# A fused attention and expert layer on one core: the shared MLP of two batches of eight moved behind the experts

## The chip, the cores and the metric

One core of a Trainium2 chip runs the whole program in one launch. The time is device microseconds (us). PE is the matmul engine, ACT (ScalarE), DVE (VectorE) and POOL (GpSimd) are the three others that compute, and SP only issues DMAs. Each engine takes its instructions in the written order, so one that waits holds up all behind it.

## The reference, cut to what matters

Eight batches of 1024 rows with 256 numbers pass through an attention layer and then this (T = 8192 rows, 16 experts, C = 1024 rows for each):

```python
    scores = jax.nn.softmax(flat_x @ gate_w.T, axis=-1).T
    topk_weight, topk_idx = jax.lax.top_k(scores, C)
    xg = flat_x[topk_idx]
    h = gelu(einsum('ecd,eid->eci', xg, Wg)) * einsum('ecd,eid->eci', xg, Wu)      # I = 1024
    eo = einsum('eci,edi->ecd', h, Wd) * topk_weight[..., None]
    flat_out = zeros_like(flat_x).at[topk_idx.reshape(-1)].add(eo.reshape(-1, d))
    shared = gelu(flat_x @ Sg.T) * (flat_x @ Su.T) @ Sd.T                          # IS = 512
    x = x + _layernorm(out + shared)
```

## The kernel before, in words

Four stages follow each other, each a block of its own with a barrier at its end: attention, the shared MLP, the experts and the output. `mlp` (line 1038) is written for both MLPs.

The shared MLP works in halves of 512 rows, 16 of them. A half has four up steps (`step`, one for 128 of the 512 hidden columns): PE makes 12 matmuls for G and U (each product in three, high and low parts of both operands), ACT takes the gelu of G, DVE multiplies it with U out of PSUM (line 1322), ACT rounds the product to its high part (1257) and DVE subtracts for the low part (1308, `part_lo`). Then `down` multiplies with Sd in four tiles of 128 rows, psD has two buffers, and ACT takes each tile out (1288). SP stores it to ACC in DRAM. The order on all engines is: steps 0 and 1, and then for each half its steps 2 and 3, steps 0 and 1 of the next half, and `down` of this one. Steps are numbered through, 64 in all.

Beside it `TopK` (line 679) finds the 1024 rows of each expert. It has a table for each engine that says after which step a piece runs. 30 bits of the threshold are found one after another: DVE counts (788), PE sums over partitions (793), DVE updates (798, 800). A count stands after each step from 3, so four in a half. At step 34 come the masks (865), then ranks (934), slots (940 to 946) and digits (951, 953) in steps 36 to 41, and from step 42 the lists: for each of eight chunks DVE writes lo1 twice (975), hi1 twice (965) and val (988, 989), POOL writes the other half of val (776), and PE multiplies them (1004). POOL then writes the lists to DRAM and reads them back as indices.

The experts stage has 16 experts with two halves each of eight up steps and a `down` of eight matmul groups per tile. POOL gathers rows by index, and adds the result to ACC with an indirect DMA for each tile (1443). SP loads the weights.

The output stage (`output`, line 1459) takes pairs of batches. SP loads F from ACC (1490). DVE takes statistics of 16 tiles (1525), aggregates them (1528) and computes scale and shift in a chain of 12 instructions on 16 numbers per partition (63 to 75, `layernorm_scale`). ACT normalises (1556), POOL adds the residual X1 in halves of 128x1024 (1569), and SP stores. The last batch is normalised and added on DVE (1543, 1546).

## Time and profile before

| what | value |
|---|---|
| time, three runs | 2233.16, 2235.63 (median), 2236.29 us |
| profiled execution, first to last instruction | 2228.4 us |
| PE busy | 2048.3 us (92%) |
| DVE, ACT, POOL busy | 1227.1, 994.6, 448.8 us |
| PE's matmuls of the shared MLP | first 688.4, last 1021.1 us |
| PE's matmuls of the experts | first 1037.8, last 2147.4 us |
| output stage | to 2228.4 us |

The profiled execution's own time outside the trace isn't given; its span stands 7.2 us under the median of the runs. Matmuls are pipelined and their listed durations overlap, so the pace of PE is read from the distance of starts. A row of a timeline with "x16" is 16 instructions merged, with the time from the first start to the last end.

### The profile page before, as it was taken

The numbers are of one execution on the slowest core, as the hardware profiler recorded it, in microseconds if no ns is written. First come the engines' busy times: TensorE is split into PE (matmuls) and PEld (weight loads), VectorE is DVE, ScalarE is ACT, GpSimd is POOL, SyncE is SP. The second block draws the span as 40 slices with busy tenths as digits, with TensorE's granted clock in tenths as the row PEclk, the third lists the DMA queues.
The fourth block names the chain that finished last, engine by engine and source line by source line (L and its number), as shares of the span: only waits on it lengthen the run. The fifth ranks groups of instructions, "written<-read, shape, count | busy, mean of one in ns | idle before, by whom it ended". The sixth has DMA issues, their size and how long they took to land. (4 is left out here: it accounts for less than half of the span.)

```text
span 2228.4 us, 34450 instructions
## 1 busy us (share of the span) xinstructions
PE 2048.3 (92%) x12462; PEld 1800.2 (81%) x12464; DVE 1227.1 (55%) x2535; ACT 994.6 (45%) x1854; POOL 448.8 (20%) x391
## 2 busy tenths in 40 slices
PE   7999999999967999886999999999999999999950
PEld 6888888888855888775888888888888888888840
DVE  5586667567564776993453443534435344353438
ACT  4464565566433434223443443434434344344415
POOL 0000000000001000233123232232322323223115
PEclk9999999999988999998999999999999999999985
DMA  2011011010013111103233333333333333333247
GB/s 107 1 39 59 39 77 58 39 56 39 40 77 124 58 56 57 38 29 137 72 75 76 88 75 76 86 62 89 75 75 85 63 87 75 76 85 63 69 113 282
DMA packets 53987, 165.74 MB, mean 74 GB/s; under 512 B 6657, under 2 KB 23233, under 8 KB 46689
## 3 DMA queue, kind: packets, MB, share of 16 engines
q1 hardware_dynamic: 29104, 129.13, 15.7%
q0 software_dynamic: 24752, 34.75, 9.7%
q8 instruction: 97, 1.59, 0.3%
q14 instruction: 34, 0.27, 0.0%
HBM read 104.55 MB, written 59.31 MB: 74 GB/s over the span
## 5 line engine op out<-in xcount | busy, mean ns | idle before, releaser
L1322 DVE TENSOR_TENSOR ex_HF<-ex_psU,ex_GL 128x512 f32<-128x512 f32 x256 | 177.1, 692 | 619.1 <-ACT ex_GL L1263 619.1
L1443 POOL DMA_INDIRECT ACC<-ex_OUT,ex_GI x128 | 200.2, 1564 | 710.0 <-ACT ex_OUT L1288 682.0
L1263 ACT ACTIVATE ex_GL<-ex_psG 128x512 f32<-128x512 f32 x256 | 153.4, 599 | 358.7 <-PE ex_psU L56 358.7
L54 PE MATMUL ex_psD<-ex_wd_hi,ex_H_hi 128*128 128x256 f32 x1024 | 289.8, 283 | 0.2 <-DVE ex_H_lo L1308 0.2
L55 PE MATMUL ex_psD<-ex_wd_lo,ex_H_hi 128*128 128x256 f32 x1024 | 289.8, 283 | 0.0
L56 PE MATMUL ex_psD<-ex_wd_hi,ex_H_lo 128*128 128x256 f32 x1024 | 289.8, 283 | 0.0
L54 PE MATMUL ex_psG<-ex_XT_hi,ex_wg_hi 128*128 128x512 f32 x512 | 206.5, 403 | 11.2 <-issue 9.7
L56 PE MATMUL ex_psG<-ex_XT_hi,ex_wg_lo 128*128 128x512 f32 x512 | 200.4, 391 | 0.0
L54 PE MATMUL ex_psU<-ex_XT_hi,ex_wu_hi 128*128 128x512 f32 x512 | 200.3, 391 | 0.0
L56 PE MATMUL ex_psU<-ex_XT_hi,ex_wu_lo 128*128 128x512 f32 x512 | 200.2, 391 | 0.0
L55 PE MATMUL ex_psG<-ex_XT_lo,ex_wg_hi 128*128 128x512 f32 x512 | 200.1, 391 | 0.0
L55 PE MATMUL ex_psU<-ex_XT_lo,ex_wu_hi 128*128 128x512 f32 x512 | 199.6, 390 | 0.0
L54 PEld LDWEIGHTS ex_psD<-ex_wd_hi,ex_H_hi 128*128 128x128 f32 x1024 | 196.4, 192 | 1.7 <-DVE ex_H_lo L1308 0.4
L55 PEld LDWEIGHTS ex_psD<-ex_wd_lo,ex_H_hi 128*128 128x128 f32 x1024 | 196.5, 192 | 1.2
L56 PEld LDWEIGHTS ex_psD<-ex_wd_hi,ex_H_lo 128*128 128x128 f32 x1024 | 196.5, 192 | 0.0
L1288 ACT ACTIVATE ex_OUT<-ex_psD,ex_TW 128x256 f32<-128x256 f32 x128 | 60.9, 476 | 278.9 <-PE ex_psD L56 278.9
L1308 DVE TENSOR_TENSOR ex_H_lo<-ex_HF,ex_H_hi 128x512 fp32r<-128x512 f32 x256 | 174.5, 682 | 0.1
L662 POOL TENSOR_TENSOR X<-X,x_a 128x1024 f32 (+1 forms) x15 | 36.3, 2422 | 620.9 <-ACT x_a L399 620.9
L1257 ACT ACTIVATE ex_H_hi<-ex_HF 128x512 fp32r<-128x512 f32 x256 | 159.7, 624 | 0.2 <-DVE ex_HF L1322 0.2
L1434 POOL DMA_INDIRECT ex_XG<-XN,ex_GI x128 | 128.7, 1005 | 48.2 <-issue 34.1
L54 PEld LDWEIGHTS ex_psG<-ex_XT_hi,ex_wg_hi 128*128 128x128 f32 x512 | 96.7, 189 | 29.5 <-issue 12.5
L56 PEld LDWEIGHTS ex_psG<-ex_XT_hi,ex_wg_lo 128*128 128x128 f32 x512 | 96.3, 188 | 21.0
(239 smaller groups left out, 5020.6 us busy)
## 6 DMA issues: line engine op xcount, KB each, us to landing
x_a<-wg_in SPq DMA_DIRECT2D x16, 1024.0 KB, 4.9
x_a<-wu_in SPq DMA_DIRECT2D x16, 1024.0 KB, 4.9
x_b<-wd_in SPq DMA_DIRECT2D x16, 1024.0 KB, 5.3
XN<-XNB SPq DMA_DIRECT2D x8, 1088.0 KB, 4.0
X<-x_in SPq DMA_DIRECT2D x8, 1024.0 KB, 6.3
X<-X SPq DMA_DIRECT2D x8, 1024.0 KB, 4.4
XN2T<-xn2T SPq DMA_DIRECT2D x8, 1024.0 KB, 3.8
ACC<-sh_OUT SPq DMA_DIRECT2D x16, 512.0 KB, 2.9
```

What stands on the lines that cost most here:

```text
L54: pe.matmul(out, w_hi, x_hi, start=first, stop=False)
L55: pe.matmul(out, w_hi, x_lo, start=False, stop=False)
L56: return pe.matmul(out, w_lo, x_hi, start=False, stop=last)
L662: g.tensor_tensor(x, x, Y[:, 4 * h:4 * h + 4, :], ALU.add).then_inc(s_x1, 1)
L1257: a.activation(H[0][:, slot(tb, it), :], HF[:, it % 2, :], ACT.Copy).then_inc(s_hhi, 1)
L1263: a.activation(GL[:, it % 2, :], psG[:, it % 2, :], ACT.Gelu).then_inc(s_gelu, 1)
L1288: a.activation(OUT[:, z, :], psD[:, t % 2, 0:D], ACT.Copy, scale=scale).then_inc(s_ev, 1)
L1308: v.tensor_tensor(H[1][:, slot(tb, it), :], HF[:, it % 2, :], H[0][:, slot(tb, it), :].bitcast(F32), ALU.subtract).then_inc(s_hlo, 1)
L1322: v.tensor_tensor(HF[:, it % 2, :], psU[:, it % 2, :], GL[:, it % 2, :], ALU.mult).then_inc(s_mul, 1)
L1434: g.indirect_dma_start(out=XG[q][:, t, :], out_offset=None, in_=io["XN"], in_offset=bass.IndirectOffsetOnAxis(ap=GI[q][:, t:t + 1], axis=0 ...
L1443: g.indirect_dma_start(out=io["ACC"], out_offset=bass.IndirectOffsetOnAxis(ap=GI[q][:, t:t + 1], axis=0), in_=OUT[:, t, :], in_offset=None ...
```

## The change

`mlp` is split into `shared_mlp`, for six batches (`NBB`), and `experts`, which takes in the output stage too; the barrier between the experts and the output is gone. In the shared stage there are 48 steps in place of 64. The threshold gets five counts per half in place of four, the other pieces of `TopK` move to earlier steps and closer together, and POOL and SP write zeros to ACC for the last two batches.

```diff
+ND = 2
+NBB = NB - ND
...
+    COUNTS = [p for s in range(2, 28, 4) for p in (s, s + 1, s + 2, s + 3, s + 3.5) if p >= 3][:NBIT]
+    INDEX = {p: i for i, p in enumerate(COUNTS)}
+    MASKS = 27
+    CHUNKS = 34
...
-        self.act = {1: [self.a_sct], M + 1: [self.a_mk], M + 2: [self.a_tot, lambda a: self.a_rank(a, (0,))],
-                    M + 3: [lambda a: self.a_rank(a, (1, 2))], M + 3.5: [lambda a: self.a_rank(a, (3,))],
-                    M + 7.5: [self.a_digits]}
-        self.pe = {1: [self.p_sct], M + 1: [self.p_masks], M + 2: [self.p_tot, lambda e: self.p_rank(e, (0,))],
-                   M + 3: [lambda e: self.p_rank(e, (1, 2))], M + 3.5: [lambda e: self.p_rank(e, (3,))]}
+        self.vec = {2: [self.v_const], M: [self.v_masks], M + 3: [self.v_prefix], M + 4: [self.v_ahead],
+                    M + 5: [self.v_rank, self.v_slot], M + 6: [self.v_slot2, self.v_digits]}
+        self.act = {1: [self.a_sct], M + 2: [self.a_mk], M + 2.5: [self.a_tot, lambda a: self.a_rank(a, (0,))],
...
+        places = [x for s in range(self.CHUNKS, 4 * self.CHUNKS) for x in [s] * (2 if s % 4 >= 2 else 1) + [s + 0.5] * (4 if s % 4 == 1 else 0)]
...
+        g.memset(self.zero, 0.0).then_inc(self.s_zero, 1)
...
+    def vec_at(self, v, x):
+        if x in self.INDEX:
+            if self.INDEX[x]:
+                self.update(v, self.INDEX[x] - 1)
+            self.count(v, self.INDEX[x])
+        if x == self.MASKS:
+            self.update(v, NBIT - 1)
+        self.run(self.vec, v, x)
...
+            if k == 0:
+                v.wait_ge(self.s_zst, 64 * ND // 2)
```

PE's sums of the counts stand between its matmuls, and SP stores the zeros:

```diff
+                    if ps is psG and s % 4 == 0:
+                        lists.pe_sum(pe, s - 2)
+                i.then_inc(s_up, 1)
+                lists.pe_at(pe, s)
+            def down(h):
+                tb, s = h % 2, NI * (h + 1) + 1
+                lists.pe_sum(pe, s - 2)
+                wait(pe, s_hlo, NI * (h + 1) - 2)
+                for t in range(4):
+                    if t == 2:
+                        lists.pe_sum(pe, s - 1)
+                    wait(pe, s_ev, EV0 + 4 * h + t - 1)
+                    for it in range(NI):
+                        if t == 0 and it >= NI - 2:
+                            wait(pe, s_hlo, NI * h + it + 1)
+                        z = slot(tb, it)
+                        i = mm3(pe, psD[:, t % 2, 0:D], H[0][:, z, t * P:(t + 1) * P], H[1][:, z, t * P:(t + 1) * P],
+                                wd[0][:, it, :], wd[1][:, it, :], it == 0, it == NI - 1)
+                    i.then_inc(s_dn, 1)
+                lists.pe_sum(pe, s)
+                if h < 2 * N - 1:
+                    lists.pe_at(pe, s + 0.5)
...
+            sp.wait_ge(lists.s_zero, 1)
+            for b in range(NBB, NB):
+                for tb in range(2):
+                    sp.dma_start(acc[b][tb], lists.zero).then_inc(lists.s_zst, 16)
+            for h in range(2 * N):
+                if h + 2 < 2 * N:
+                    load(h + 2)
+                store(h)
+            for tb in range(2):
+                sp.wait_ge(s_st[tb], 16 * N)
+                sp.wait_ge(c.s_raw[tb], 16)
+            sp.wait_ge(lists.s_zst, 32 * ND)
```

Behind the last up step of the last expert come four halves of the shared MLP (`d` 0 to 3, batches 6 and 7) in the same pattern. The last expert's `down` stands behind the first two of their steps. The weights Sg, Su and Sd are loaded again and split during the last expert. F and X1 lie over buffers that are free by then. The output is taken in 16 halves (`HALVES`) with seven chains (`GROUP` names the chain that a batch waits for).

```diff
+        GROUP = {0: 1, "d0": 1, 1: 2, "d1": 3, 2: 3, 3: 4, "d2": 5, 4: 5, 5: 6, "d3": 7}
+        HALVES = [(0, 0), (0, 1), ("d0", 0), (1, 0), (1, 1), ("d1", 0), (2, 0), (2, 1), (3, 0), (3, 1), ("d2", 0), (4, 0), (4, 1),
+                  (5, 0), (5, 1), ("d3", 0)]
...
+        def shared_schedule(step, down, last_down):
+            for it in range(2):
+                step(0, it)
+            last_down()
+            for d in range(DB):
+                for it in range(2, NJ):
+                    step(d, it)
+                if d < DB - 1:
+                    for it in range(2):
+                        step(d + 1, it)
+                down(d)
+        def final(n):
+            return isinstance(n, int) and n == N - 1
...
+            def shared_step(d, it):
+                if d == 0 and it == 0:
+                    pe.wait_ge(s_dlo, 3)
+                if it == 0:
+                    wait(pe, s_xlo, 2 * (LAST + 2 + d))
+                wait(pe, s_mul, NI * 2 * N + NJ * d + it - 1)
+                up(it, d % 2, dsw["g"], dsw["u"])
+            def shared_down(d):
+                wait(pe, s_hlo2, NJ * (d + 1) - 2)
+                for t in range(4):
+                    if d == 0 and t < 2:
+                        wait(pe, s_ev, EV0 + 4 * (LAST + 1) + t - 1)
+                    else:
+                        wait(pe, s_evd, 4 * d + t - 1)
+                    for it in range(NJ):
+                        if t == 0 and it >= NJ - 2:
+                            wait(pe, s_hlo2, NJ * d + it + 1)
+                        z = slot(d % 2, it)
+                        i = mm3(pe, psD[:, t % 2, 0:D], H[0][:, z, t * P:(t + 1) * P], H[1][:, z, t * P:(t + 1) * P],
+                                dsw["d"][0][:, it, :], dsw["d"][1][:, it, :], it == 0, it == NJ - 1)
+                    i.then_inc(s_dn, 1)
```

ACT normalises one tile at a time between its other work:

```diff
+            def shared_step(d, it):
+                gelu(NI * (LAST + 1) + NJ * d + it, it)
+                if it:
+                    shared_part_hi(d, it - 1)
+                elif d == 0:
+                    part_hi(LAST, 1, NI - 1)
+                else:
+                    shared_part_hi(d - 1, NJ - 1)
+                if it < 2 and d < DB - 1:
+                    shared_x_hi(d + 1, it)
+                if d == 2 and it < 2:
+                    normalize(0, range(2 * it, 2 * it + 2))
+                if d == 2 and it >= 2:
+                    normalize(1, range(2 * it - 4, 2 * it - 2))
+                if d == 3 and it < 2:
+                    normalize(1, range(2 * it + 4, 2 * it + 6))
+                if d == 3 and it == 2:
+                    normalize(2, (6, 7))
+                if d == 3 and it == 3:
+                    normalize(3, (0, 1))
+            def shared_down(d):
+                if d == 1:
+                    normalize(0, range(4, 8))
+                    normalize("d0", range(4))
+                if d == 2:
+                    normalize("d1", range(4))
+                    normalize(2, range(6))
+                if d == 3:
+                    shared_part_hi(d, NJ - 1)
+                    normalize(3, range(2, 8))
+                    normalize("d2", range(4))
+                    normalize(4, range(8))
+                    normalize(5, range(8))
+                    normalize("d3", range(2))
```

DVE takes `down`'s tiles out of PSUM and adds them to F, which it also does the statistics of:

```diff
+            def stats(u, ts):
+                wait(v, s_f[u], 16)
+                for t in ts:
+                    v.bn_stats(st[:, BASE[u] + t, :], f_tile(u, t))
+            def add_tile(d, t):
+                u = f"d{d}"
+                if t == 0:
+                    if d < 2:
+                        wait(v, s_f[u], 16)
+                    else:
+                        wait(v, s_f["d23"], 16)
+                wait(v, s_dn, 4 * (LAST + 1 + d) + t + 1)
+                v.tensor_tensor(f_tile(u, t), psD[:, t % 2, 0:D], f_tile(u, t), ALU.add).then_inc(s_evd, 1)
+                v.drain()
+                v.bn_stats(st[:, BASE[u] + t, :], f_tile(u, t))
+            def aggregate(z, n):
+                v.drain()
+                for t in range(z, z + n):
+                    v.bn_aggr(mv[:, t, :], st[:, t, :])
+            def chain(z, n):
+                v.drain()
+                for part in range(2):
+                    i = layernorm_scale(v, part, mv[:, z:z + n, :], ve[:, z:z + n], rs[:, z:z + n], shift[:, z:z + n], tmp[:, z:z + n], n)
+                i.then_inc(s_r, 1)
+            for quarter in range(4):
...
+            def shared_step(d, it):
+                k = NJ * d + it
+                wait(v, s_gelu, NI * (LAST + 1) + k + 1)
+                if k < 2:
+                    wait(v, s_hlo, NI * (LAST + 1) + k - 1)
+                else:
+                    wait(v, s_hlo2, k - 1)
+                v.tensor_tensor(HF[:, it % 2, :], psU[:, it % 2, :], GL[:, it % 2, :], ALU.mult).then_inc(s_mul, 1)
+                if k == 0:
+                    part_lo(LAST, 1, NI - 1)
+                if it < 2 and d < DB - 1:
+                    shared_x_lo(d + 1, it)
+                if d == 1 and it == 1:
+                    stats(0, range(4))
+                if d == 1 and it == 2:
+                    chain(0, 12)
+                if d == 1 and it == 3:
+                    stats(1, range(4))
+                if d == 2 and it == 0:
+                    stats(1, range(4, 8))
+                if d == 2 and it == 1:
+                    aggregate(12, 8)
+                    chain(12, 8)
+                if d == 2 and it == 2:
+                    chain(20, 12)
+                if d == 2 and it == 3:
+                    stats(3, range(4))
+                if d == 3 and it == 0:
+                    stats(3, range(4, 8))
+                if d == 3 and it == 1:
+                    aggregate(32, 8)
+                    chain(32, 8)
+                if d == 3 and it == 2:
+                    chain(40, 12)
+                if d == 3 and it == 3:
+                    stats(5, range(8))
+                    aggregate(52, 8)
+            def shared_down(d):
+                if d == 0:
+                    stats(0, range(4, 8))
+                if d == 1:
+                    stats(2, range(4))
+                if d == 2:
+                    stats(4, range(4))
+                if d == 3:
+                    chain(52, 8)
+                for t in range(4):
+                    add_tile(d, t)
+                if d == 0:
+                    aggregate(0, 12)
+                if d == 1:
+                    stats(2, range(4, 8))
+                    aggregate(20, 12)
+                if d == 2:
+                    stats(4, range(4, 8))
+                    aggregate(40, 12)
+                if d == 3:
+                    aggregate(60, 4)
+                    chain(60, 4)
+                    v.drain()
+                    for t in (2, 3):
+                        v.tensor_scalar(f_tile("d3", t), f_tile("d3", t), rs[:, 60 + t:61 + t], shift[:, 60 + t:61 + t], ALU.mult, ALU.add)
+                    v.drain()
+                    f, x = f_half("d3", 0), x1_half(NB - 1, 1)
+                    wait(v, s_x1[NB - 1], 16)
+                    v.tensor_tensor(f[:, 2:4, :], f[:, 2:4, :], x[:, 2:4, :], ALU.add).then_inc(s_lastn, 1)
```

SP loads F when all scatters have landed. The low parts of H are POOL's in this stage, and so are the residuals:

```diff
+            sp.wait_ge(s_dlo, 3)
+            load_x1(2)
+            load_x1(3)
+            sp.wait_ge(s_xhi, 2 * (LAST + 2))
+            sp.wait_ge(s_xlo, 2 * (LAST + 2))
+            load_x(2)
+            sp.wait_ge(s_xhi, 2 * (LAST + 3))
+            sp.wait_ge(s_xlo, 2 * (LAST + 3))
+            load_x(3)
+            sp.wait_ge(s_up, 2 * NI * N)
+            sp.wait_ge(s_dn, 8 * N)
+            for q in range(2):
+                sp.wait_ge(s_sc[q], 64 * N)
+            load_f(0)
             for h in range(2):
-                for t in range(4 * h, 4 * h + 4):
-                    v.tensor_scalar(F[:, b, t, :], F[:, b, t, :], rs[:, p, NT + t:NT + t + 1], shift[:, p, NT + t:NT + t + 1],
-                                    ALU.mult, ALU.add)
-                v.drain()
-                v.tensor_tensor(half(F, b, h), half(F, b, h), half(xb, 1, h), ALU.add).then_inc(s_al, 1)
...
+                    sp.wait_ge(s_add, first + 1)
+                    sp.dma_start(rows_of(io["out"], b)[:, h, :], f_half(u, 0).rearrange("p j c -> p (j c)")).then_inc(s_out, 16)
+                else:
+                    sp.wait_ge(s_add, first + 2)
+                    sp.dma_start(rows_of(io["out"], u), two(F[u][:, :, :])).then_inc(s_out, 16)
+            store(0)
+            load_x1(NB - 1)
+            for u in ("d0", 1, "d1", 2, 3, "d2", 4, 5):
+                store(u)
+            for k, (s, value) in enumerate(((s_add, len(HALVES)), (s_lastn, 1))):
+                sp.wait_ge(s, value)
+                sp.dma_start(rows_of(io["out"], NB - 1)[:, 1, 2 * k * D:(2 * k + 2) * D],
+                             f_half("d3", 0)[:, 2 * k:2 * k + 2, :].rearrange("p j c -> p (j c)")).then_inc(s_out, 16)
...
+            def part_lo(d, it):
+                wait(g, s_hhi, NI * (LAST + 1) + NJ * d + it + 1)
+                z = slot(d % 2, it)
+                g.tensor_tensor(H[1][:, z, :], HF[:, it % 2, :], H[0][:, z, :].bitcast(F32), ALU.subtract).then_inc(s_hlo2, 1)
+            def residual(i):
+                u, h = HALVES[i]
+                b, z = rows_at(u, h)
+                wait(g, s_n, i + 1)
+                wait(g, s_x1[b], 32 if b == 5 else 16)
+                n = 2 if u == "d3" else 4
+                g.tensor_tensor(f_half(u, h)[:, 0:n, :], f_half(u, h)[:, 0:n, :], x1_half(b, z)[:, 0:n, :], ALU.add).then_inc(s_add, 1)
+            for d, it in ((0, 0), (0, 1)):
+                part_lo(d, it)
+            scatter(N - 1, 1, 1)
+            for d, it in ((0, 2), (0, 3), (1, 0), (1, 1), (1, 2), (1, 3), (2, 0), (2, 1)):
+                part_lo(d, it)
+            residual(0)
+            part_lo(2, 2)
+            residual(1)
+            part_lo(2, 3)
+            residual(2)
+            part_lo(3, 0)
+            part_lo(3, 1)
+            residual(3)
+            residual(4)
+            part_lo(3, 2)
+            residual(5)
+            part_lo(3, 3)
+            for i in range(6, len(HALVES)):
+                residual(i)
 class Consts:
     pass
```

## Rows read from the trace of the kernel before

**Rows 1.** Windows: us, then busy of PE, PEld, DVE, ACT, POOL, clock, DMA.
```profile
707.00:842.00 135.00, 135.00 (x804) 119.74 (x803) 94.49 (x198) 52.73 (x107) 0.00 (x0) 1.00 0.18 63
842.00:883.40 41.40, 39.18 (x228) 32.18 (x229) 25.09 (x42) 20.76 (x39) 0.00 (x0) 1.00 0.15 51
883.40:992.40 109.00, 98.77 (x631) 83.59 (x630) 103.83 (x102) 32.66 (x63) 31.79 (x7) 0.98 0.10 35
2163.10:2228.40 65.30, 0.00 (x0) 0.00 (x0) 56.39 (x186) 28.01 (x56) 32.89 (x14) 0.50 0.78 299
```

**Rows 2.** Timeline, DVE, shared stage: start us, us, operation.
```profile
706.94 0.69 DVE L1238 TENSOR_TENSOR sh_XT_lo<-XR,sh_XT_hi 128x512 fp32r<-128x512 f32 x1
...
812.86 0.69 DVE L1238 TENSOR_TENSOR sh_XT_lo<-XR,sh_XT_hi 128x512 fp32r<-128x512 f32 x1
...
841.97 0.75 DVE L865 TENSOR_SCALAR sh_val<-sh_SCT,sh_cand 128x1024 bf16<-128x1024 f32 x1
...
872.42 0.69 DVE L1322 TENSOR_TENSOR sh_HF<-sh_psU,sh_GL 128x512 f32<-128x512 f32 x1
...
873.03 0.68 DVE L1308 TENSOR_TENSOR sh_H_lo<-sh_HF,sh_H_hi 128x512 fp32r<-128x512 f32 x1
...
883.39 1.22 DVE L975 TENSOR_TENSOR sh_lo<-sh_LO,sh_VI 128x2048 bf16<-128x2048 bf16 x1
...
990.03 2.35 DVE L965 TENSOR_TENSOR sh_hi<-sh_HI,sh_VI 128x2048 bf16<-128x2048 bf16 x2
...
1015.34 0.29 DVE L1023 SCALAR_TENSOR_TENSOR sh_LS<-sh_vu,sh_vj 128x128 int32<-128x128 int32 x1
```

**Rows 3.** Timeline, ACT, last expert.
```profile
2132.97 0.60 ACT L1263 ACTIVATE ex_GL<-ex_psG 128x512 f32<-128x512 f32 x1 [1.60 <-PE ex_psU L56]
...
2135.69 0.60 ACT L1263 ACTIVATE ex_GL<-ex_psG 128x512 f32<-128x512 f32 x1 [1.60 <-PE ex_psU L56]
...
2139.11 0.47 ACT L1288 ACTIVATE ex_OUT<-ex_psD,ex_TW 128x256 f32<-128x256 f32 x1 [1.43 <-PE ex_psD L56]
...
2141.99 0.47 ACT L1288 ACTIVATE ex_OUT<-ex_psD,ex_TW 128x256 f32<-128x256 f32 x1 [2.40 <-PE ex_psD L56]
```

**Rows 4.** Timeline and transfers: last scatter, first load of F.
```profile
2149.01 1.56 POOL L1443 DMA_INDIRECT ACC<-ex_OUT,ex_GI  x1 [1.32 <-ACT ex_OUT L1288]
...
DMA to landing us min/median/max: 3.6/3.8/5.1
...
2157.77 5.70 SPq L1490 DMA_DIRECT2D F<-ACC  x3
...
out_dram<-F SPq DMA_DIRECT2D x4, 512.0 KB, 2.8
```

**Rows 5.** Timeline, DVE, output stage.
```profile
2163.11 5.33 DVE L1525 BATCH_NORM_STATS2 fst<-F 128x6 f32<-128x256 f32 x16 [24.70 <-DMA F<-ACC]
...
2168.51 1.17 DVE L1528 BATCH_NORM_AGGREGATE fmv<-fst 128x2 f32<-128x6 f32 x16
...
2172.87 0.18 DVE L75 SCALAR_TENSOR_TENSOR fsh<-fmv,frs 128x16 f32<-128x16 f32 x1 [0.43 <-issue]
...
2179.88 2.35 DVE L63 TENSOR_SCALAR fve<-fmv 128x16 f32<-128x16 f32 x1
...
2218.58 5.43 DVE L1543 TENSOR_SCALAR F<-F,frs,fsh 128x256 f32<-128x256 f32 x4
```

**Rows 6.** Timeline, POOL, output stage.
```profile
2175.25 9.25 POOL L1569 TENSOR_TENSOR F<-F,x_a 128x1024 f32<-128x1024 f32 x4 [24.68 <-ACT F L1556]
```

**Rows 7.** Timeline, POOL and then DVE, attention.
```profile
289.12 2.41 POOL L662 TENSOR_TENSOR X<-X,x_a 128x1024 f32 x1 [70.27 <-ACT x_a L399]
...
290.25 0.47 DVE L607 SCALAR_TENSOR_TENSOR O_lo<-psL,rinv,O_hi 128x256 fp32r<-128x256 f32 x1
```

**Rows 8.** Windows, PE alone: us, busy, granted clock, DMA.
```profile
939.00:941.00 2.00, 0.23 (x2) 0.87 0.00 0
941.00:943.00 2.00, 2.00 (x11) 0.50 0.00 0
```

More of the change, by code:

```diff
@@ L1289, in down @@
[L1289 to L1295 removed]
+                    if t == 0 and tb == 0:
+                        wait(a, s_tw, n + 1)
+                        wait(a, s_sc[1 - q], 64 * (n - q) + 128 * q)
+                    a.activation(OUT[:, z, :], psD[:, t % 2, 0:D], ACT.Copy, scale=TW[q][:, z:z + 1]).then_inc(s_ev, 1)
@@ L1336, in down @@
[L1336 to L1345 removed]
+                    w_lo(task[0], n + task[1], (q + task[1]) % 2, task[2])
```

762 lines of the change are left out of this document (404 added, 358 removed).

## The prediction

> **What bounds the kernel now.** First the table of busy time: PE 92%. Then the windows by stage, which show where PE is not the bound. In the shared stage PE is busy through the 135 us of the threshold search and 39.2 of the next 41.4 us. In the stretch of the lists it is busy 98.8 of 109.0 us and DVE 103.8, so DVE sets the pace there. In the output stage PE has nothing for 65.3 us while DVE is busy 56.4 [rows 1]. The change puts PE work into that hole. The chain of waits that ended last also lies on DVE in the output stage. The question is thus what PE's work costs DVE and POOL, which carry the output.
>
> **The shared stage, four terms.** The span is 2228.4 us; I reckon against it and add the difference to the median at the end.
>
> Pace of PE. An up step of 12 matmuls takes 2135.69 − 2132.97 = 2.72 us. A tile of an expert's `down`, 24 matmuls, takes 2.88 us, thus 0.12 each [rows 3]. A shared tile has 12, so 1.44 us, and a half 4 x 2.72 + 4 x 1.44 = 16.6 us. Four halves are 66.6 us, the most the stage can shrink by. Measured, six halves took 812.86 − 706.94 = 105.9 us, 17.65 each [rows 2]: each of the four sums costs PE 0.25.
>
> 1. *To the masks.* From the x_lo of step 4 (706.9) to the masks was 135.0 us. Now 23 steps lie between, not 30: five halves at 16.6 + 5 x 0.25 = 17.9, then a `down` of 5.8, three steps and their sums, 9.7: 105. Masks at 812: 30 us earlier. Bounds: 28 to 30.5; at 28 every half loses 0.4 us to the fifth count, as DVE's update and count are queued behind three 0.6 us instructions and PE's last sum waits for them.
> 2. *Masks to the first lo1.* It was 41.4 us [rows 1] for eight steps, now seven: 38.7. But ranks, slots and digits are now in two adjacent steps, 32 and 33, and `a_digits` stands on ACT ahead of the evictions of a `down`. PE fills two psD buffers and then waits for ACT, which waits for DVE. I take 8 us, bounds 0 and 10 (all of these DVE instructions, a third of the 25.1 us of DVE time in this window, in PE's way). 46.7, so lo1 at 859.
> 3. *The lists.* They took 109.0 us with 18 products, 18 low parts and 8 x_lo of the shared MLP in them, at 0.61 us each (873.03 − 872.42) [rows 2]. Now steps 35 to 47 lie there: 13, 13 and 4. 14 fewer save 8.5 us on DVE, the bound; 2 come back as waits, since PE too is near its bound. 102.5: the last hi1 ends at 961.5. Bounds: 98 and 109.
> 4. *To the end of the lists.* Before, 992.4 to 1015.6, as the last pieces waited for steps. Now nothing separates them: POOL's value 4.5 (31.79/7 [rows 1]), DVE's 2.3 ahead of it, 32 matmuls 3.9, decoding 2: 12.7. PE idles about 10 us before; the granted clock was 0.50 (1.2 GHz) after 2 us with 0.23 us of work [rows 8], so 3 us more: 15.7. Lists ready at 977.
>
> Gain 1015.6 − 977 = 38.5 us, bounds 28 and 48. Behind it come the stores of the lists, barrier and gather as before. PE has finished its halves by then. The four zero stores (2 MB) replace four stores of OUT; they wait in SP's queue behind 2 MB of weights, ahead of the next x load. That load has more than 10 us until PE needs it, so nothing; if it were late, 3 us.
>
> **The experts** stay as they are, 0. The splitting of the shared weights adds three instructions each to ACT and DVE in the last expert, where both idle over half the time (1.60 us before each gelu [rows 3]); bounds 0 and 3.
>
> **The tail.** I count from the end of the last expert's last up step, 2135.5 in the old trace. Before, 92.9 us followed.
>
> *When F arrives.* Two shared steps 5.4, the last `down` 11.5: 2152.4. POOL's scatters stand behind `part_lo(0,1)`, whose high part ACT makes only behind the four evictions and the gelu of step (0,2): 2.7 + 1.2, then 1.2 on POOL (half of 9.25/4 = 2.31 [rows 6]). Four scatters at 1.56 + 0.3, the last landing 3.8 after its issue, and an F load of 5.3 from issue to DVE's first statistics [rows 4, 5]: 2172.9. Before it was 2163.1. DVE stands at `stats(0)` for that long, and PE, which needs DVE to empty psD, with it.
>
> *DVE's work from there:* 64 statistics at 0.333, 21.3; 64 aggregates at 0.073, 4.7; seven chains at 3.3 (from the end of the aggregates, 2169.7, to 2172.87 + 0.18), 23.1 [rows 5]; ten products and two x_lo at 0.61, 7.3; 16 tiles out of PSUM at 0.54 (0.47 in the row, with a drain [rows 7]), 8.6; the last two tiles 1.5. Sum 66.5 us. PE has from then about 40 us to do, so DVE is the bound.
>
> *Collisions.* A POOL instruction holds up DVE ones that read two SBUF operands, and `tensor_scalar`: the `ve` at 2179.88 took 2.35 us in place of 0.18, as POOL ran. There are six such in the chains (2.13 to 2.35), two short ones, and 5.43 in place of 1.4 us for the last batch: 16.8 us in all [rows 5] against 14 x 2.31 = 32.4 us of POOL [rows 6], 52%. Statistics, and reads from PSUM, go undisturbed: 0.47 us at 290.25, inside a POOL instruction [rows 7]. New on POOL are 12 low parts and 15.5 residuals in the time, 49.8 us; 52% is 26 us. Bounds 0 and 37 (every POOL instruction that is ready in a chain goes between two of its steps).
>
> The page "SBUF — State Buffer" of the Trainium skill, section "SBUF: two separate sides", has this as an exclusive lock: whichever instruction starts first has the shared ports for its whole length. That speaks against moving low parts to POOL beside seven chains. By it alone the ceiling is all 49.8 us of POOL and the time some 24 us later than forecast; the rows of the output stage bear the lock out, but only at half that share.
>
> *Waits of DVE.* DVE is in order: in each `down` it waits for each tile (1.44 against 0.87 of work, 2.3 a half, 9 in all), and after each stall of PE for the next gelu (2.7, some three times). 15 us, bounds 5 and 20.
>
> End of DVE: 2172.9 + 66.5 + 26 + 15 = 2280.4. The last store lands 2.8 us behind, with the issue 3.4 [rows 4]: 2283.8, so 55.4 us later than 2228.4.
>
> **Sum.** −38.5 + 55.4 = +16.9; 2245.3 us in the trace. That stands to the median of the runs, 2235.6, as the old span does, 7.2 us under it: 2252.5.
>
> **Rivals.**
>
> *Fewer collisions (the other side, faster).* Between the tail's fixed part (2172.9 + 66.5 + 3.4 = 2242.8, +14.4) and the gain of 38.5 lie 24.1 us. If collisions and waits together are below that, the kernel is faster. For it: the interleaving on POOL puts the low parts before chains and could keep both apart; against it, POOL's residuals become ready exactly when a chain has ended, and chains follow each other. With no collisions and 10 us of waits: 2242.8 + 10 − 38.5 = 2214.3, and the time 2221.5.
>
> *PE is the bound.* The tail would be 11.5 + 66.6 and about 9 for the closing chain: 2222.6, and the time 2191. Against it: DVE's sum alone ends later.
>
> *Collisions and clock together (slower still).* DVE's stalls leave PE idle for 4 to 8 us in each half, and the clock then halves, as it did at 941 [rows 8]. Some 10 us of PE's 66.6 doubled, and collisions at 37: +21, the time 2273.5.
>
> *The stage does not shrink.* DVE-bound, with term 3 at 109 and term 2 at its end: gain 30; the time 2261.
>
> **Chances.** Forecast with its neighbourhood (2238 to 2268) 0.50; fewer collisions 0.25, PE-bound 0.05; collisions and clock 0.10; no shrinking 0.10. A measurement here tells 0.2% (4.5 us). The lower edge of the forecast's case and the upper of the first rival's meet there. Faster by more: 0.28, same: 0.07, slower: 0.65. The range is 2210 to 2273: the lower end takes in most of the first rival, the upper the third. The forecast's own range is 2238 to 2268.
>
> **What would show it.** The last `LS` of the lists near 977, the first F statistics 37 us behind the last expert's last up step, the chains on DVE with instructions of 1.2 and 2.3 us between those of 0.18, PE idle before the third tile of `down` in each shared half, and a `down` of batch 7 that waits for POOL's low parts behind residuals. I am wrong if PE is busy through the tail, or if the chains stay at 3.2 us.

## The result: slower by 1.15%, where 0.8% was forecast

The kernel after takes 2260.86 us (median of 4 runs, 2257.67 to 2262.78), the kernel before beside it 2235.23 (4 runs, 2233.16 to 2236.29): ratio 1.0115, 95% interval [1.0101, 1.0130]. 2252.5 was forecast, range 2210 to 2273.

In the traces the span goes from 2228.4 to 2255.8 us. Three stretches carry the 27.4 us:

| stretch | forecast | measured |
|---|---|---|
| to the first matmul of the experts (1037.82, now 998.62) | −38.5 | −39.2 |
| experts, to the gelu of the last own up step (2135.69, now 2100.22) | 0 | +3.7 |
| tail, from that gelu to the end (92.7, now 155.6) | +55.4 | +62.9 |

**The profile after.** The windows first (us, busy of PE, PEld, DVE, ACT, POOL with their instructions, granted clock of PE, DMA), for the stretches of [rows 1]: search, masks to the first lo1, and lists; then the tail.

```profile
707.00:809.30 102.30, 102.30 (x612) 91.22 (x611) 81.23 (x174) 39.27 (x79) 0.00 (x0) 1.00 0.18 62
809.30:858.60 49.30, 39.04 (x216) 32.26 (x215) 23.85 (x38) 19.32 (x37) 0.00 (x0) 0.86 0.13 44
858.60:964.00 105.40, 87.64 (x564) 75.44 (x563) 100.87 (x91) 25.27 (x50) 30.99 (x7) 0.93 0.07 26
...
2132.00:2161.00 29.00, 22.76 (x112) 19.89 (x111) 20.41 (x57) 8.94 (x17) 6.78 (x6) 0.78 0.84 326
2161.00:2187.00 26.00, 14.59 (x63) 12.62 (x64) 19.99 (x67) 9.41 (x20) 7.53 (x5) 0.84 0.12 38
2187.00:2222.00 35.00, 20.41 (x98) 17.89 (x97) 27.20 (x86) 15.18 (x31) 16.74 (x10) 0.74 0.24 93
2222.00:2243.00 21.00, 6.84 (x33) 6.54 (x32) 17.48 (x18) 10.10 (x21) 17.58 (x9) 0.50 0.44 175
```

PE is full in the search, and has 10 us of holes in the 49.3 behind the masks, where it had 2 in 41.4. In the tail PE is busy 56 to 78% at first and a third of the time at the end, while DVE is busy 70 to 83%. The search is PE's, the lists and the tail are not.

The shared stage on DVE (start, us), answering to [rows 2]: masks, the first lo1, the last hi1, the last LS. 812, 859, 961.5 (its end) and 977 were forecast.

```profile
809.27 0.75 DVE L859 TENSOR_SCALAR sh_val<-sh_SCT,sh_cand 128x1024 bf16<-128x1024 f32 x1
...
858.64 2.36 DVE L971 TENSOR_TENSOR sh_lo<-sh_LO,sh_VI 128x2048 bf16<-128x2048 bf16 x2
...
962.73 1.22 DVE L959 TENSOR_TENSOR sh_hi<-sh_HI,sh_VI 128x2048 bf16<-128x2048 bf16 x1
...
977.14 0.29 DVE L1019 SCALAR_TENSOR_TENSOR sh_LS<-sh_vu,sh_vj 128x128 int32<-128x128 int32 x1
```

How F arrives, from ACT, POOL, SP and DVE of the same trace: the gelu from which the tail is counted, the high part of step (0,1), which ACT makes behind the gelu of step (0,2), POOL's low part that waited for it, the last scatter, the load, the first statistics. They come 36.9 us behind the gelu; 37.4 was forecast.

```profile
2100.22 0.60 ACT L1506 ACTIVATE ex_GL<-ex_psG 128x512 f32<-128x512 f32 x1 [1.60 <-PE ex_psU L58]
...
2120.42 0.62 ACT L1553 ACTIVATE ex_H_hi<-ex_HF 128x512 fp32r<-128x512 f32 x1
...
2121.12 1.28 POOL L1914 TENSOR_TENSOR ex_H_lo<-ex_HF,ex_H_hi 128x512 fp32r<-128x512 f32 x1 [12.96 <-ACT ex_H_hi L1553]
...
2128.15 1.56 POOL L1899 DMA_INDIRECT ACC<-ex_OUT,ex_GI  x1 [0.30 <-issue]
...
2131.99 0.37 SPq L1796 DMA_DIRECT2D ex_F<-ACC  x1
...
2137.14 2.71 DVE L1669 BATCH_NORM_STATS2 ex_st<-ex_F 128x6 f32<-128x256 f32 x8 [2.67 <-DMA ex_F<-ACC]
```

A chain for batches that come later: ACT, then DVE with the product ahead of the chain, then POOL, in the same microseconds. [Rows 5] have a chain instruction alone at 0.18 us.

```profile
2205.53 0.60 ACT L1506 ACTIVATE ex_GL<-ex_psG 128x512 f32<-128x512 f32 x1 [8.14 <-PE ex_psU L58]
2206.02 0.62 ACT L1553 ACTIVATE ex_H_hi<-ex_HF 128x512 fp32r<-128x512 f32 x1
...
2206.16 0.69 DVE L1712 TENSOR_TENSOR ex_HF<-ex_psU,ex_GL 128x512 f32<-128x512 f32 x1 [0.17 <-ACT ex_GL L1506]
2206.95 1.10 DVE L65 TENSOR_SCALAR ex_ve<-ex_mv 128x12 f32<-128x12 f32 x1
2208.12 2.25 DVE L67 TENSOR_SCALAR ex_rs<-ex_ve 128x12 int32<-128x12 int32 x1
2210.45 2.22 DVE L70 TENSOR_TENSOR ex_tmp<-ex_rs 128x12 f32<-128x12 f32 x1
2212.74 1.14 DVE L72 SCALAR_TENSOR_TENSOR ex_tmp<-ex_tmp,ex_ve 128x12 f32<-128x12 f32 x1
2213.96 2.23 DVE L74 SCALAR_TENSOR_TENSOR ex_rs<-ex_tmp,ex_rs 128x12 f32<-128x12 f32 x1
2216.27 0.17 DVE L70 TENSOR_TENSOR ex_tmp<-ex_rs 128x12 f32<-128x12 f32 x1
...
2206.72 1.29 POOL L1914 TENSOR_TENSOR ex_H_lo<-ex_HF,ex_H_hi 128x512 fp32r<-128x512 f32 x1 [13.85 <-ACT ex_H_hi L1553]
2207.97 4.67 POOL L1923 TENSOR_TENSOR ex_F<-ex_F,ex_XG 128x1024 f32<-128x1024 f32 x2
2212.59 1.26 POOL L1914 TENSOR_TENSOR ex_H_lo<-ex_HF,ex_H_hi 128x512 fp32r<-128x512 f32 x1
2213.82 2.35 POOL L1923 TENSOR_TENSOR ex_F_d<-ex_F_d,x_b 128x1024 f32<-128x1024 f32 x1
```

In this chain exactly one of DVE's instructions goes through for each of POOL's, and it lasts as long as POOL's: 1.1 us beside a low part, 2.2 beside a residual of 1024 columns. The rows also show why the two meet. The gelu at 2205.53 releases DVE's product, with the chain behind it. On ACT the high part of the step before stands right behind the same gelu, it releases POOL's low part, and the residuals stand behind that in POOL's queue. So POOL's burst and DVE's chain are released together.

### The profile page after: what moved, and what is told of

It reads as the page before. It is cut to its first block, busy times and chain, and to the rows that moved or that the text cites. A ratio compares the mean times of both kernels' runs of the same rounds, so it can differ in the third digit from the quotient of the medians.

```text
span 2255.8 us, 34184 instructions
## 1 busy us (share of the span) xinstructions
PE 2072.2 (92%) x12464; PEld 1822.8 (81%) x12464; DVE 1249.7 (55%) x2565; ACT 993.9 (44%) x1847; POOL 474.5 (21%) x410
## 4 chain that ended last, share of the span: by engine, by line
PE 50%; issue 3%; POOL 2%; DVE 1%; DMA 1%; ACT 0%; DVEq 0%; POOLq 0%; SPq 0%
PE ex_psG L56 5%; PE ex_psD L56 5%; PE ex_psD L57 5%; PE ex_psD L58 5%; PE ex_psG L58 5%; PE ex_psG L57 5%; PE ex_psU L56 5%; PE ex_psU L58 5%; PE ex_psU L57 5%; PE ex_psXT L1387 1%; POOL ex_F L1923 1%; DMA ex_F<-ACC 0%; POOL ex_F_d L1923 0%; POOL ex_H_lo L1914 0%; POOL ex_XG L1890 0%
## 5 line engine op out<-in xcount | busy, mean ns | idle before, releaser
L1506 ACT ACTIVATE ex_GL<-ex_psG 128x512 f32<-128x512 f32 x272 | 162.8, 598 | 411.6 <-PE ex_psU L58 411.6
L56 PE MATMUL ex_psG<-ex_XT_hi,ex_wg_hi 128*128 128x512 f32 x544 | 220.6, 406 | 18.4 <-issue 9.8
L58 PE MATMUL ex_psG<-ex_XT_hi,ex_wg_lo 128*128 128x512 f32 x544 | 214.1, 394 | 0.0
L57 PE MATMUL ex_psG<-ex_XT_lo,ex_wg_hi 128*128 128x512 f32 x544 | 213.9, 393 | 0.0
L56 PE MATMUL ex_psU<-ex_XT_hi,ex_wu_hi 128*128 128x512 f32 x544 | 213.6, 393 | 0.0
L58 PE MATMUL ex_psU<-ex_XT_hi,ex_wu_lo 128*128 128x512 f32 x544 | 213.2, 392 | 0.0
L57 PE MATMUL ex_psU<-ex_XT_lo,ex_wu_hi 128*128 128x512 f32 x544 | 212.7, 391 | 0.0
L56 PEld LDWEIGHTS ex_psG<-ex_XT_hi,ex_wg_hi 128*128 128x128 f32 x544 | 103.5, 190 | 38.8 <-issue 12.7
L58 PEld LDWEIGHTS ex_psG<-ex_XT_hi,ex_wg_lo 128*128 128x128 f32 x544 | 103.1, 190 | 22.6
```

The lines of the kernel that those rows point to most:

```text
L56: pe.matmul(out, w_hi, x_hi, start=first, stop=False)
L57: pe.matmul(out, w_hi, x_lo, start=False, stop=False)
L58: return pe.matmul(out, w_lo, x_hi, start=False, stop=last)
L1506: a.activation(GL[:, it % 2, :], psG[:, it % 2, :], ACT.Gelu).then_inc(s_gelu, 1)
```

## The experiments

All but the last start from the kernel after. "Excess" is what DVE's instructions behind F last beyond the shortest of their form in any of these traces, "F" is from the gelu above to the first statistics, "DVE" from there to DVE's last end, and "close" from there to the end of the span.

| kernel | median us | ratio to before | tail | F | DVE | excess | close |
|---|---|---|---|---|---|---|---|
| after | 2260.86 | 1.0115 | 155.6 | 36.9 | 112.9 | 30.2 | 5.8 |
| chains in PSUM | 2241.16 | 1.0027 [1.0017, 1.0037] | 136.5 | 37.0 | 91.4 | 6.8 | 8.2 |
| scatter first | 2255.18 | 1.0092 [1.0077, 1.0108] | 151.1 | 30.8 | 114.4 | 30.2 | 5.8 |
| digits later | 2248.80 | 1.0064 [1.0051, 1.0078] | 154.8 | 36.7 | 112.2 | 30.2 | 5.8 |
| residual of 4 columns | 2232.19 | 0.9988 [0.9979, 0.9997] | 127.6 | 36.8 | 85.9 | 6.7 | 4.8 |
| the first three together | 2225.82 | 0.9960 [0.9947, 0.9974] | 128.8 | 30.8 | 94.4 | 10.6 | 3.5 |
| low parts on DVE | 2247.61 | 1.0054 [1.0041, 1.0068] | 145.0 | 30.3 | 108.8 | 22.5 | 5.8 |
| low parts on DVE, chains in PSUM, digits later | 2219.01 | 0.9926 [0.9913, 0.9940] | 124.3 | 30.3 | 90.2 | 5.7 | 3.8 |
| and the first moved batch first | 2217.20 | 0.9921 [0.9908, 0.9935] | 121.5 | 30.8 | 86.8 | 5.0 | 3.9 |
| and two chains fewer | 2214.33 | 0.9912 [0.9897, 0.9927] | 117.5 | 30.8 | 82.8 | 5.1 | 3.9 |
| before, chains in PSUM | 2224.62 | 0.9956 [0.9942, 0.9969] | 82.4 | – | – | – | – |

**Chains in PSUM.**

```diff
-                for part in range(2):
-                    i = layernorm_scale(v, part, mv[:, z:z + n, :], ...)
-                i.then_inc(s_r, 1)
+                pv, py = psX[:, 0, 0:n], psX[:, 0, 64:64 + n]
+                ys, t = rs[:, z:z + n], tmp[:, z:z + n]
+                v.tensor_scalar(pv, mv[:, z:z + n, 1], EPS, None, ALU.add)
...
+                for _ in range(3):
+                    v.tensor_tensor(t, ys, py, ALU.mult)
+                    v.drain()
+                    v.scalar_tensor_tensor(t, t, -0.5, pv, ALU.mult, ALU.mult)
+                    v.drain()
+                    v.scalar_tensor_tensor(ys, t, 1.5, py, ALU.add, ALU.mult)
+                    v.scalar_tensor_tensor(py, t, 1.5, py, ALU.add, ALU.mult)
+                    v.drain()
```

> The kernel after the change, with one edit: the intermediates of DVE's LayerNorm chains lie in PSUM, so that no instruction of a chain after the change reads two operands from SBUF (four instructions more in each chain, 16 in place of 12). Theory T (the tail is DVE's queue, and POOL stretches the chains in it): the excess of the chains, 29.4 us in the kernel after the change, falls to 0 to 8 us; the four added instructions cost 7 to 8 chains x 4 x 0.2 to 0.28 = 6 to 8 us; the sum is 13 to 23 us less on DVE, of which some comes back as waits for PE's tiles. Tail 10 to 18 us shorter, time 2243 to 2251 us. Rival A (PE is held by POOL's low parts behind residuals, and DVE only waits for PE): the chains shrink, DVE's waits grow by the same amount, time 2258 to 2263. Rival B (the exclusion holds for every DVE instruction, PSUM operand or not): the chains stay at 2.2 us an instruction wherever POOL runs and get longer by the four, time 2266 to 2275.

19.7 us less in the median, 19.1 in the tail, a little more than theory T expected, since the added instructions cost some 0.09 us each and not 0.2: two writes of the same result need no drain between them. The chains have no excess left; the 6.8 us lie in the last two tiles' normalizing and residual (5.6) and in x_lo (1.1), which were left in SBUF. DVE and POOL in this kernel, in one stretch:

```profile
2205.48 0.17 DVE L1703 SCALAR_TENSOR_TENSOR ex_rs<-ex_tmp,ex_psXT 128x12 f32<-128x12 f32 x1
2205.56 0.17 DVE L1704 SCALAR_TENSOR_TENSOR ex_psXT<-ex_tmp,ex_psXT 128x12 f32<-128x12 f32 x1
...
2203.82 4.67 POOL L1936 TENSOR_TENSOR ex_F<-ex_F,ex_XG 128x1024 f32<-128x1024 f32 x2
```

The same chain, under the same residuals, runs at 0.17 us an instruction. The Trainium skill's page "SBUF — State Buffer", section "Who interferes with whom", says that a DVE instruction with at most one SBUF input, outside of the two-port modes, doesn't contend with GpSimd; the trace agrees. Rival B falls. Rival A falls too: DVE's waits for tiles and gelus did not grow by what the chains lost (15.9 us after, 14.6 here, and 1.4 for a low part), and PE's waits in the tail, by the waits of either trace (in total, times, longest), get shorter with the chains. After, and then this kernel:

```profile
PE ex_psD L56 <- DVE ex_F_d L1680: 28.5, 4, 14.2
PE ex_psD L56 <- POOL ex_H_lo L1914: 13.1, 4, 5.7
PE ex_psG L56 <- DVE ex_HF L1712: 7.1, 2, 5.6
```

```profile
PE ex_psD L56 <- DVE ex_F_d L1680: 15.3, 3, 6.2
PE ex_psD L56 <- POOL ex_H_lo L1927: 10.7, 5, 4.9
```

PE waited for DVE, and DVE for POOL's lock.

**The second scatter first.**

```diff
-            for d, it in ((0, 0), (0, 1)):
-                part_lo(d, it)
+            part_lo(0, 0)
             scatter(N - 1, 1, 1)
-            for d, it in ((0, 2),
+            for d, it in ((0, 1), (0, 2),
```

> The kernel after the change, with one edit: on POOL the last expert's second scatter stands ahead of the low part of step (0,1), not behind it. Theory T (the late F opens DVE's queue late): the scatters follow the evictions at 2108.5 to 2117.2 in place of 2122.6 to 2128.2, F's first statistics come 8 to 10 us earlier (2127 to 2129 in place of 2137.1), and DVE, whose queue sets the end, ends 5 to 10 us earlier: time 2251 to 2256. Rival A (PE's 16 steps and 4 downs with POOL's low parts are the queue that sets the end): F is earlier by as much, and DVE waits longer for gelus and tiles; time within 3 us of 2261.

F comes 6.1 us earlier, not 8 to 10: a scatter can't start before its own eviction, and the last of those starts at 2117.2. The tail gets 4.5 us shorter, the median 5.7. The time is in theory T's range, at the low end of its gain (DVE is through 4.6 us sooner, where 5 to 10 were expected), and outside rival A's.

**Digits later.**

```diff
-                    M + 6: [self.a_digits]}
+                    M + 6.5: [self.a_digits]}
```

> The kernel after the change, with one edit: in the shared stage ACT's digits stand half a step later in its queue, behind the evictions of the down that they stood ahead of. Theory T (term 2 of the prediction: PE waits 9.5 us at this place, and this delays the first lo1): PE's wait is gone or under 2 us, the lists are ready 5 to 9 us earlier, time 2252 to 2256. Rival (DVE's own work sets the pace of the stretch, the 9.5 us are in its shadow, or the later digits delay the first product of the lists by as much): the wait of PE moves to another line, the lists are ready within 2 us of 977, time 2259 to 2262.

12.1 us less in the median, 3 more than the top of what was expected. What it repairs, in the kernel after (ACT's digits, its evictions, and PE's matmul behind them), and the same place in this kernel:

```profile
845.83 1.06 ACT L952 ACTIVATE sh_LO<-sh_SCT 128x1024 bf16<-128x1024 int32 x1 [8.32 <-DVE sh_SCT L947]
...
847.73 0.64 ACT L1154 ACTIVATE sh_OUT<-sh_psD 128x256 f32<-128x256 f32 x2
...
848.15 0.58 PE L56 MATMUL sh_psD<-sd,sh_H_hi 128*128 128x256 f32 x1 [9.45 <-ACT sh_OUT L1154]
```

```profile
841.06 0.38 ACT L1154 ACTIVATE sh_OUT<-sh_psD 128x256 f32<-128x256 f32 x1 [1.06 <-PE sh_psD L58]
845.26 1.06 ACT L952 ACTIVATE sh_LO<-sh_SCT 128x1024 bf16<-128x1024 int32 x1 [3.82 <-DVE sh_SCT L947]
...
848.99 1.22 DVE L971 TENSOR_TENSOR sh_lo<-sh_LO,sh_VI 128x2048 bf16<-128x2048 bf16 x1
```

The digits themselves come at the same time (845.3 and 845.8), since DVE decides on that. What was lost was ACT's 8.3 us of standing still with PE's two full buffers behind it. Masks to the first lo1: 49.4 us after, 40.3 here. The first matmul of the experts comes 10.6 us earlier; the rival falls.

**A residual of four columns.** It leaves out the rest of POOL's residual additions.

```diff
-                g.tensor_tensor(f_half(u, h)[:, 0:n, :], f_half(u, h)[:, 0:n, :], x1_half(b, z)[:, 0:n, :], ALU.add)...
+                g.tensor_tensor(f_half(u, h)[:, 0:n, 0:4], f_half(u, h)[:, 0:n, 0:4], x1_half(b, z)[:, 0:n, 0:4], ALU.add)...
```

> The kernel after the change, with one edit: POOL's residuals add only 4 of the 256 columns, so that each takes some 0.2 us and not 2.3 (the rest of the residual is left out; all waits and orders stay). Theory T: most of the 30 us of collisions on DVE go with them (36 of the 50 us of POOL in this time), 20 to 27 us; PE's waits for POOL's low parts (13.1 us) go too, in the shadow of DVE's queue. The low parts of POOL still collide, 4 to 8 us. Some comes back as waits for PE: time 2236 to 2246. Rival A (POOL only occupies its own queue, DVE's slow instructions are in the shadow): the gain is that of the last residual and of the waits for low parts alone, 3 to 9 us, time 2252 to 2258. Rival B (PE at half its clock sets the end): the gain is under 5 us.

28.7 us less, 28.0 in the tail, more than any other single edit. DVE's excess falls by 23.5 us; what stays in the chains are single instructions of 1.1 us beside a low part. The 3.8 us beyond the expected range are there because DVE's waits for tiles and gelus fell too, by 3.5 us, where I expected them to grow; PE's waits for POOL's low parts went from 13.1 to 7.6 us and those for DVE's adding from 28.5 to 16.8. Both rivals fall: they allowed 9 and 5 us.

**The three repairs together.**

> The kernel after the change, with the three edits of the runs before together: chains' intermediates in PSUM, the last expert's second scatter ahead of POOL's low part of step (0,1), ACT's digits half a step later. Alone they gave 19.7, 5.7 and 12.1 us in the medians. Theory T (the stage and the tail are separate, and in the tail the late F and the collisions are terms of one queue on DVE): they add up to within 4 us, 37.5 us in all, time 2220 to 2228, which is faster than the kernel before by 0.3 to 0.7%. Rival (with the collisions gone POOL's queue of low parts and residuals, or PE, ends last): the gain of the earlier scatter is gone, time 2228 to 2233, no faster than before by more than 0.3%.

35.0 us less against a sum of 37.5 of the three. They add up, and the kernel is faster than before by 0.4% [0.26, 0.53].

Of the 10.6 us of excess that are left, 9.5 lie in one instruction: the first of DVE's two normalizings of the last tiles. POOL's residuals stand in its queue without a gap there, DVE and then POOL:

```profile
2205.47 10.27 DVE L1780 TENSOR_SCALAR ex_F_d<-ex_F_d,ex_rs,ex_shift 128x256 f32<-128x256 f32 x2
...
2204.78 4.67 POOL L1936 TENSOR_TENSOR ex_F<-ex_F,ex_OUT 128x1024 f32<-128x1024 f32 x2
2209.38 4.66 POOL L1936 TENSOR_TENSOR ex_F<-ex_F,ex_X 128x1024 f32<-128x1024 f32 x2
```

The first of the two lasts 9.95 us and the second 0.40. It outlasts four residuals and the half-size one behind them, which ends at 2215.27, so one POOL instruction's length is not the most that a DVE instruction can lose. What decides whether DVE gets its turn between two of POOL's stays open.

**Low parts on DVE.**

```diff
+            def shared_part_lo(k):
+                wait(v, s_hhi, NI * (LAST + 1) + k + 1)
+                z = slot(k // NJ % 2, k % NJ)
+                v.tensor_tensor(H[1][:, z, :], HF[:, k % 2, :], H[0][:, z, :].bitcast(F32), ALU.subtract).then_inc(s_hlo2, 1)
...
                 if k == 0:
                     part_lo(LAST, 1, NI - 1)
+                else:
+                    shared_part_lo(k - 1)
...
+            scatter(N - 1, 1, 1)
+            for i in range(len(HALVES)):
+                residual(i)
```

> The kernel after the change, with one edit: DVE makes the low parts of the two moved batches (16 at about 0.65 us), right behind the next product, and POOL has the scatters and the residuals alone. The chains stay in SBUF. Theory T (DVE's queue is the bound in the tail): DVE gets 10.4 us more; it loses a third of its collisions at most (12 to 16 of POOL's low parts at 1.2 us of 50 us in all, 5 to 8 us, since residuals then meet the chains more often) and the 7.1 us that it waits for POOL's low part behind the scatters; F comes 6 us earlier as in the run with the scatter first (4.5 us of gain). Sum -4 to +2: time 2252 to 2263. Rival A (PE is held by POOL's low parts behind residuals, 13.1 us of waits): these waits are on the path that sets the end, time 2243 to 2250.

13.3 us less in the median, 10.6 in the tail. By its time this is rival A; DVE's rows add up without it. F comes 6.6 us earlier, and DVE's stretch behind it is 4.1 us shorter: 11 of the 16 low parts fall there, 11 x 0.6 = 6.9 us more; the excess is 7.7 lower, inside the 5 to 8 expected; and its waits for gelus and tiles are 3.0 lower. I had charged all 16 low parts, but five stand where DVE waits for F anyway, and had F's gain too small. Most of PE's waits didn't go: 33.1 us for DVE's adding out of psD (28.5 in the kernel after), 8.6 for low parts (13.1) and 0.4 for products (7.1), 42.1 in all against 48.7. So rival A isn't excluded by this run; how much of the gain is PE's isn't separated. The chain shown above, and POOL, in this kernel:

```profile
2207.80 0.17 DVE L65 TENSOR_SCALAR ex_ve<-ex_mv 128x12 f32<-128x12 f32 x1
2208.05 2.31 DVE L67 TENSOR_SCALAR ex_rs<-ex_ve 128x12 int32<-128x12 int32 x1
...
2207.95 2.37 POOL L1931 TENSOR_TENSOR ex_F<-ex_F,x_a 128x1024 f32<-128x1024 f32 x1 [14.20 <-ACT ex_F L1559]
```

One residual meets this chain in place of three with two low parts. Without low parts ahead of them, residuals run when ACT has made them ready. It moves the collisions more than it removes them: the next chain still meets four (seven in the kernel after).

**All of it, low parts on DVE.**

> All together, but with the low parts of the moved batches on DVE: chains in PSUM, digits later, POOL only with scatters and residuals. Against the kernel with the three edits: Theory T (DVE's queue, now without collisions, is still what ends last): 10.4 us more on DVE less some 8 us of waits for low parts: within 3 us of it or up to 3 slower. Rival A (POOL's queue: in the run with the chains in PSUM alone POOL was busy without a gap from 2201.1 to the end, DVE had ended at 2232.4 of 2240.6): POOL is relieved of 12 low parts, the end comes 4 to 8 us earlier, time 2213 to 2221.

2219.0 us, 6.8 less than the three repairs: in the range of rival A, not of theory T. The tail is 4.5 us shorter; where the rest of the 6.8 comes from is not shown. DVE has 11 low parts more behind F, and its stretch is yet 4.2 us shorter: its waits fall by 5.5 us (for PE's tiles 11.8 to 7.7, for POOL's low parts 1.4 to none), and the last two tiles' normalizing takes 3.5 us and not 10.3, since POOL's queue has run down by then.

**The first moved batch first.**

```diff
                 if d == 0:
+                    stats(0, range(8))
                     aggregate(0, 12)
...
-            load_f(0)
             for h in range(2):
                 sp.dma_start(F[NBB][:, 4 * h:4 * h + 4, :]..., rows_of(io["ACC"], NBB)[:, h, :]).then_inc(s_f[f"d{h}"], 16)
+                if h == 0:
+                    load_f(0)
```

> The kernel with low parts on DVE, chains in PSUM and digits later, with one more edit: DVE adds the first moved batch's tiles out of PSUM ahead of the statistics of F's first batch (8 at 0.33 us), and the load of the F rows that this takes is issued ahead of the first batch's. Theory T (F's late arrival holds DVE, and PE with it through two full PSUM buffers): PE goes on 2.7 us plus up to 1.5 us of transfer earlier, the end 2 to 5 us earlier than without this edit. Rival (PE's stall there is in the shadow of DVE's sum of work, which is the same): within 1.5 us of the kernel without it.

1.8 us less in the median, 2.8 in the tail; the intervals of the two ratios overlap, so this is not settled.

**Two chains fewer.** Chains of 8 and 12 columns become one of 20, twice.

> The fastest kernel so far (chains in PSUM, digits later, low parts on DVE, first moved batch ahead of F's first statistics: 2217.2 us) with two chains of 8 and 12 columns made one of 20, twice. An instruction of 8 columns takes 0.16 us and one of 20 hardly more, so a chain costs its count of instructions. Theory T (DVE's queue still sets the end): two chains of 3.4 us go, 6.8 us less on DVE, the end 4 to 7 us earlier, time 2210 to 2213. Rival (ACT's and POOL's work becomes ready too late: the normalizing of 8 tiles that chain 2 released now waits some 12 us for the joint chain, and POOL, busy without a gap from 2191.3 to 2209.3 in that kernel, ends last): within 2 us of 2217.

2.9 us less (tail 4.0), below what theory T expected (4 to 7) and above the rival's 2: 2.8 of the 6.8 us that DVE was spared came back as waits. Again the intervals overlap. The sum of all edits is sure: 2214.3 us is 0.9% under the kernel before [0.73, 1.03], the fastest kernel here.

**The kernel before, chains in PSUM.**

> The kernel before the change, with the one edit that helped most after it: the four LayerNorm chains of the output stage have their intermediates in PSUM. Theory T (the output stage of the kernel before is DVE's queue too, and its chains contain 12.8 us of excess under POOL's residuals: 4.1, 4.1 and 4.5 us): the stage gets 8 to 12 us shorter, time 2223 to 2227. That would leave the moved MLP, with its own repairs at 2217.2, an advantage of 6 to 10 us of its own. Rival (POOL's residuals, 2.31 us each behind ACT, or the stores set the end of that stage): under 4 us, time 2231 to 2235.

9.6 us less (0.44% [0.31, 0.58]), in the range of theory T. The chain of its second pair, which took 7.2 us in the kernel before (from 2179.88, with 2.35 and 2.13 in it, to 2187.12), stands under 9.26 us of POOL that began at 2181.59:

```profile
2186.23 0.18 DVE L1534 TENSOR_SCALAR fpsN<-fmv 128x16 f32<-128x16 f32 x1
...
2189.48 0.17 DVE L1547 SCALAR_TENSOR_TENSOR fsh<-fmv,fpsN 128x16 f32 x1 [0.16 <-issue]
```

The chain now takes 3.4 us. So some 10 of the 20 us between the kernel before and the fastest one can be had by an edit that has nothing to do with the move. The move and its other repairs bring the rest, 10.3 us between the two kernels with this edit; whether fewer chains would help the kernel before as well wasn't tried.

## Why the prediction was right, and where its terms were off

The signs that the prediction named were there: the last `LS` at 977, F 36.9 us behind the gelu, chain instructions of 1.1 and 2.2 us between those of 0.17, PE waiting for DVE in each `down` (4.4, 5.9, 4.1 and 14.2 us), and the first `down` of batch 7 waiting for a low part behind residuals (4.9 us).

*To the masks*: 809.3 against 812, 2.7 us earlier. Of these 1.6 lie ahead of the point from which I counted (the x_lo of step 4 starts at 705.3, not 706.9), which no term was about; a half took 17.8 us, where 17.9 was charged. *Masks to lo1*: 49.4 against 46.7, 0.7 above the upper bound of 38.7 + 10. The mechanism that I named (`a_digits` ahead of a `down`'s evictions) was there to the row, with 9.45 us of PE's wait; I took 8. The run with the digits later puts its price at 9.1 us up to lo1 and 10.6 at the first matmul of the experts, and without it the stretch takes 40.3, not 38.7.

*The lists*: 105.3 against 102.5. DVE was the bound, as said, but it was busy 100.9 us where the prediction's own subtraction (103.8 − 8.5) leaves 95.3. What the prediction did not look at is that this stretch has collisions too: POOL writes its half of val, 4.1 to 5.1 us each time, and DVE's instructions last longer under it. Over the whole stretch they last 27.0 us beyond the shortest of their form, and 23.5 in the kernel before. DVE and POOL in the kernel after; the same DVE instruction takes 1.27 us alone:

```profile
878.48 5.23 DVE L984 TENSOR_SCALAR sh_val<-sh_hi,sh_pcol 128x4096 bf16<-128x4096 bf16 x1
...
878.52 4.10 POOL L775 TENSOR_TENSOR sh_val<-sh_hi,sh_TV 128x2048 bf16<-128x2048 bf16 x1 [9.90 <-DVE sh_hi L959]
```

That is nearly as much as in the tail of the kernel after, and no run here tried to remove it. PE's waits for low parts (9.8 us in all) are in the shadow of DVE's queue, which stood idle 4.5 us (5.2 before). *To the end of the lists*: 13.5 against 15.7. The errors of the four terms, −2.7, +2.7, +2.8 and −2.2, cancel; that the sum of the stage came out within a microsecond is luck.

*F*: 36.9 against 37.4. *DVE*: 112.9 against 107.5. By its rows that is 65.4 of own work (66.5), 17.1 of waits (15) and 30.2 of collisions (26). The items of the waits add up to 9.2 + 8.1 = 17.3, so with its own items the prediction would have had them right. The collisions were the one term with wide bounds (0 to 37). The share of 52%, carried over from the output stage, came near the 61% measured (30.2 of POOL's 49.2 us), and the order of POOL's queue decided that, so this too is in part luck. The share is not a property of the chip: 30.2 became 22.5 with 14 us of low parts gone from POOL, and 6.8 with nothing gone from it. *The close*: 5.8 against 3.4, as the last half's residual waits for ACT and POOL behind DVE.

The rivals: without collisions in the chains the tail ends 19 us sooner, yet even then the kernel is no faster than before (1.0027). The rival had 10 us of waits and 3.4 us for the close; there were 17 of waits, 8.2 for the close and 6.8 of excess outside the chains. PE-bound: PE waits for DVE and POOL 48.7 us in the tail. The clock: it is low in the tail (0.50 in 2222 to 2243), but with the chains in PSUM the tail loses 19 us and the clock stands at 0.78 to 0.87 in the windows from F's arrival to PE's end, so the lowest clock went with the waits. What the low clock costs by itself wasn't measured.

*The frame.* 2245.3 was forecast for the span and it was 2255.8, 10.5 more: 7.5 from the tail, 3.7 from the experts, −0.7 from the stage. The 7.2 us that I added to come to the median were too many: it stands 5.1 us above this span, so the median missed by 8.4. Of a run's time only 1.9 us lie outside its span (2257.67 against 2255.8 in one execution). The rest was that the profiled execution of before had been a quick one, as the last section shows.

## What to carry to other kernels

Work moved into another stage's hole has to be charged for what it does to the engines that already set that stage's end. A POOL instruction beside a chain of short DVE instructions can cost its whole length, once for each, however short those are, and several in a row can hold a single one (9.95 us, where it takes 0.40 alone); put one operand of such a chain in PSUM, or look at what releases POOL's burst. And when tables by step are shifted against each other, look on every engine for an instruction that now stands ahead of evictions and waits for a slower engine: here half a step was worth 12 us, a third of the stage's gain. And when a collision is found in one stage, look for it in every stage that the same engine bounds: here the lists had 24 to 27 us of it that nobody had counted.
